# Moving VectorE's join to the head of its step, taking the edge spans apart amid the first keys, and zeroing the row table later

## What is computed

```python
xn = layernorm(x)
# graph part: mean over the incoming edges (sorted by dst), times W
h = segment_sum((xn @ W + b)[src], dst, N) / max(deg, 1)
# linear attention over all nodes, 8 heads
q, k = elu(xn @ wq + bq) + 1, elu(xn @ wk + bk) + 1
v = xn @ wv + bv
mix = ((q @ (k.T @ v)) / (q @ k.sum(0))) @ wo + bo
x = x + h + mix
# top-1 mixture of 8 experts, each with room for 977 rows
y = expert_of_argmax(softmax(layernorm(x) @ gate_w + gate_b))
x = x + y          # relu(x_e @ w1 + b1) @ w2 + b2, times the probability
```

## Time and profile before

| | |
|---|---|
| median of 3 runs | 1361.61 us (1361.3 to 1364.84) |
| the profiled execution, its own time | 1366.44 us |
| its span, first to last instruction | 1364.7 us |
| busy PE, VectorE, ACT, POOL | 1082.8, 821.7, 545.6, 918.9 us |
| mean granted TensorE clock | 0.918 |

### The profile page before, as it was taken

How to read it: one execution, slowest core, us unless ns; L and a number is a source line. 1 busy time by engine, 2 the same in 40 slices (tenths; PEclk the granted TensorE clock), 3 DMA queues, 4 the chain that set the end, 5 groups by cost and what they waited for, 6 DMA issues and landing times.

```text
span 1364.7 us, 31269 instructions
## 1 busy us (share of the span) xinstructions
PE 1082.8 (79%) x5701; PEld 775.4 (57%) x5702; DVE 821.7 (60%) x2770; ACT 545.6 (40%) x1411; POOL 918.9 (67%) x965
## 2 busy tenths in 40 slices
PE   3769986768767777878888888888888888888895
PEld 2446654435544545556555655666665666557785
DVE  6754433557657666657566666566666666667443
ACT  4832211223323333334244444355445444555442
POOL 4646777777777776777767777777776666651741
PEclk9569988788879898989799999899999999999998
DMA  7594333445445555556555565566666655653762
GB/s 231 179 287 133 102 105 107 144 120 154 149 143 157 151 159 172 154 154 191 155 178 185 176 185 181 164 205 191 183 185 189 201 174 168 180 177 109 241 208 82
DMA packets 141586, 228.92 MB, mean 168 GB/s; under 512 B 29601, under 2 KB 86594, under 8 KB 141489
## 3 DMA queue, kind: packets, MB, share of 16 engines
q0 software_dynamic: 42800, 115.65, 28.2%
q1 hardware_dynamic: 97454, 111.65, 26.4%
q10 hardware_dynamic: 1234, 0.66, 0.2%
HBM read 194.77 MB, written 34.81 MB: 168 GB/s over the span
## 4 chain that ended last, share of the span: by engine, by line
issue 24%; DVE 23%; PE 21%; POOL 14%; DVEq 8%; DMA 4%; ACT 3%; SPq 1%; POOLq 1%; ACTq 0%
POOL shared L600 13%; PE pA L943 4%; PE pY L1067 4%; PE pH L1076 4%; DVE shared L1451 2%; DMA shared<-table,idx 2%; DVEq L1399 2%; PE pH L917 2%; DVEq L1404 2%; DMA shared<-in_L_ffn_w_dram 1%; PE pQ L990 1%; PE pD L1004 1%; PE pT L998 1%; DVE stats L1524 1%; DVE shared L1585 1%
## 5 line engine op out<-in xcount | busy, mean ns | idle before, releaser
L600 POOL DMA_INDIRECT shared<-table,idx x784 | 765.9, 977 | 277.5 <-issue 238.9
L943 PE MATMUL pA<-shared,onehot 128*128 x976 | 264.4, 399 | 110.7 <-issue 53.1
L943 PEld LDWEIGHTS pA<-shared,onehot 128*128 x976 | 92.4, 99 | 262.9 <-issue 209.5
L1391 DVE TENSOR_TENSOR onehot<-tile_iota,dst_t 128x512 f32 x244 | 159.9, 694 | 101.8 <-PE pA L943 65.2
L1067 PE MATMUL pY<-w2s,shared 128*128 x832 | 197.3, 391 | 10.9 <-issue 10.6
L1076 PEld LDWEIGHTS pH<-shared 128*128 128x128 f32 x1664 | 193.9, 192 | 7.3 <-DMA shared<-in_L_ffn_w_dram 4.7
L1076 PE MATMUL pH<-shared 128*128 128x128 f32 x1664 | 195.2, 275 | 3.3 <-DMA shared<-in_L_ffn_w_dram 3.3
L1067 PEld LDWEIGHTS pY<-w2s,shared 128*128 128x128 f32 x832 | 157.1, 194 | 34.8 <-issue 14.5
L788 ACT ACTIVATE shared<-pH,b1s 128x128 f32<-128x128 f32 x416 | 116.5, 374 | 84.8 <-PE pH L1076 73.2
L1451 DVE RECIPROCAL shared<-shared 128x256 f32<-128x256 f32 x49 | 85.9, 1753 | 36.3 <-ACT shared L738 32.5
L558 POOL DMA_INDIRECT rows<-rows_sb,row_at x49 | 52.1, 1063 | 73.1 <-issue 72.5
(11 more groups left out here) (252 smaller groups left out, 1681.9 us busy)
## 6 DMA issues: line engine op xcount, KB each, us to landing
shared<-in_L_ffn_w_dram SPq DMA_DIRECT2D x104, 512.0 KB
shared<-table,idx POOLq DMA_INDIRECT x784
w2s<-in_L_ffn_w_dram SPq DMA_DIRECT2D x8, 1024.0 KB, 7.1
rows<-rows_sb SPq DMA_DIRECT2D x7, 1040.0 KB, 14.1
shared<-rows SPq DMA_DIRECT2D x52, 130.0 KB
shared<-in_L_ffn_b_dram SPq DMA_DIRECT2D x52, 128.0 KB
shared<-in_x_dram SPq DMA_DIRECT2D x12, 512.0 KB, 8.4
table<-w2s SPq DMA_DIRECT2D x12, 512.0 KB, 4.4
```

The costliest lines, as they stand in the source:

```text
L600: g.indirect_dma_start(gathered[:, s * G + j, :], None, table[:, :], bass.IndirectOffsetOnAxis(ap=idx[:, q * G % IDX + j:q * G % IDX + j + ...
L943: m = pe.matmul(pA[:, :], one_of[j][:, bass.ds(one, P)], got_of[j][:, bass.ds(got, 2 * D)], start=False, stop=final and j == G - 1)
L1391: v.tensor_tensor(onehot[:, n % OQ, :, :], tile_iota[:, :].rearrange("p (a n) -> p a n", a=1).broadcast_to([P, G, P]), dst_t[:, bass.ds(ch ...
```

## The change

It does four things. PE opens the first four gather groups as soon as the tiles are turned, projects three tiles, and only then takes part in the edge spans, now in pD and pA; VectorE does the keys of tiles 0 and 1 in the middle of that chain; tile 0's sum is set up at tile 9 of the keys, and VectorE's first one-hots come one at a time at tiles 7, 8 and 9 instead of four at once. SP issues the zeroing behind `bob` and `xres`, and VectorE waits for it at step 2. The join becomes a function of its own, ahead of `next_tile`.

```diff
# SP
+            sp.wait_ge(S["ms_ok"], 2)
+            sp.dma_start(bob, bo.partition_broadcast(P)).then_inc(S["bo_in"], 16)
+            sp.dma_start(xres, x_t[0, :, :]).then_inc(S["xr_in"], 16)
             sp.wait_ge(S["rows_z"], 2)
             for i in range(1, NX):
                 sp.dma_start(rows_t[...], empty...).then_inc(S["zeroed"], 16)
-            (the same three lines, here)
# PE
-            the span products in pX and pT; pe.wait_ge(S["spans_ok"], 1)
+            pe.sem_inc(S["slots"], FIRST)
...
-                sum_start(load_span(0))
-                sum_zero()
                 for t in range(KB - 1):
                     project(t)
+                the span products in pD and pA
                 for t in range(NT):
+                    if t == RING_X - 2:
+                        pe.wait_ge(S["spans_ok"], 1)
+                        sum_start(load_span(0))
+                        sum_zero()
# VectorE
             v.sem_inc(S["e_lohi"], 1)
+            v.wait_ge(S["tab_st"], 16 * BATCHES)
+            keys(0, 0)
+            keys(1, 1)
             v.wait_ge(S["e_rowps"], 1)
...
+                def join(t):
+                    v.wait_ge(S["ah_ok"], t + 1)
+                    hold(v, "dve_hold")
+                    v.tensor_tensor(ss[:, 0:D], pA[:, D:2 * D], ss[:, 0:D], ALU.add).then_inc(S["join_ok"], 1)
...
                         late()
+                    if joined(t):
+                        join(t)
                     if inner or t + 1 < NT:
                         next_tile(t)
...
-                load_ends(0)
-                early()
-                v.wait_ge(S["tab_st"], 16 * BATCHES)
-                for t in range(NT + 2):
+                for t in range(2, NT + 2):
+                    if t == 5:
+                        load_ends(0)
+                        v.reg_mov(mid_r, v.snap(first_r))
+                    if t in (7, 8, 9):
+                        some()
...
-                v.wait_ge(S["zeroed"], 16 * (NX - 1))
-                v.wait_ge(S["scat_done"], 16)
...
+                    if t == 2:
+                        v.wait_ge(S["zeroed"], 16 * (NX - 1))
+                        v.wait_ge(S["scat_done"], 16)
```

More of the change, by code:

```diff
@@ L362, in _ @@
                              empty.rearrange("p (a d) -> p a d", a=1).broadcast_to([P, JOBS, ROW])).then_inc(S["zeroed"], 16)
-            sp.wait_ge(S["ms_ok"], 2)
-            sp.dma_start(bob, bo.partition_broadcast(P)).then_inc(S["bo_in"], 16)
-            sp.dma_start(xres, x_t[0, :, :]).then_inc(S["xr_in"], 16)
             def load_res(i, last=False):
@@ L880, in _ @@
                     ins.then_inc(S["gc_ps"], 1)
[L883 to L894, removed]
             gp = (pH0, pH1)
@@ L902, in _ @@
             pe.wait_ge(S["w_late"], 16 * 4)
-            pe.wait_ge(S["spans_ok"], 1)
+            pe.sem_inc(S["slots"], FIRST)
             def project(t):
@@ L920, in _ @@
             pe.sem_inc(S["kv_used"], KB)
-            pe.sem_inc(S["slots"], FIRST)
             pe.sem_inc(S["oh_slots"], OQ - 1)
@@ L1129, in step @@
                         sum_rest()
-                sum_start(load_span(0))
-                sum_zero()
                 for t in range(KB - 1):
                     project(t)
+                pe.wait_ge(S["e_bound"], 1)
+                for a in range(2):
+                    ins = pe.transpose(pD[0:NT, a * P:(a + 1) * P], bounds[:, a, :], ident[:, :])
+                ins.then_inc(S["e_bt"], 1)
+                pe.wait_ge(S["e_lohi"], 1)
+                for a in range(2):
+                    ins = pe.matmul(pA[0:1, a * 64:a * 64 + NT], lohi[:, a:a + 1], ident[0:NT, 0:NT], start=True, stop=True)
+                ins.then_inc(S["e_rowps"], 1)
+                pe.wait_ge(S["e_row"], 1)
+                pe.matmul(pD[0:NT, 0:1], new_row[0:1, 0:NT], ident[0:1, 0:1], start=True, stop=True).then_inc(S["e_newps"], 1)
+                pe.wait_ge(S["e_new"], 1)
+                pe.matmul(pA[0:1, 0:NT], new_col[:, :], tri[0:NT, 0:NT], start=True, stop=True).then_inc(S["e_baseps"], 1)
                 for t in range(NT):
+                    if t == RING_X - 2:
+                        pe.wait_ge(S["spans_ok"], 1)
+                        sum_start(load_span(0))
+                        sum_zero()
                     if t + KB - 1 < NT:
@@ L1314, in _, with keys @@
             c(v.tensor_tensor(xgs[:, :, :], xgs[:, :, :], spread(gcon[:, 1, :]), ALU.add))
+            def keys(t, b):
+                v.wait_ge(S["k_ps"], t + 1)
+                c.mark(v.scalar_tensor_tensor(xgs[:, t, :], keys_ps(t)[:, D:GW], std[:, t:t + 1], xgs[:, t, :], ALU.mult, ALU.add))
+                v.tensor_tensor(kb[:, b, :], keys_ps(t)[:, 0:D], bks, ALU.add).then_inc(S["kb_ok"], 1)
             m0 = sel_f[:, 0:NT * EBLK].rearrange("p (t b) -> p t b", b=EBLK)
@@ L1335, in _ @@
             v.wait_ge(S["e_bt"], 1)
-            c.mark(v.tensor_reduce(lohi[:, 0:1], pX[0:NT, 0:P], AX, ALU.min))
-            c(v.tensor_reduce(lohi[:, 1:2], pX[0:NT, P:2 * P], AX, ALU.max))
+            c.mark(v.tensor_reduce(lohi[:, 0:1], pD[0:NT, 0:P], AX, ALU.min))
+            c(v.tensor_reduce(lohi[:, 1:2], pD[0:NT, P:2 * P], AX, ALU.max))
             c(v.tensor_scalar(lohi[:, 0:1], lohi[:, 0:1], BIG, float(EC - 1), ALU.add, ALU.min))
@@ L1346, in _ @@
             v.sem_inc(S["e_lohi"], 1)
+            v.wait_ge(S["tab_st"], 16 * BATCHES)
+            keys(0, 0)
+            keys(1, 1)
             v.wait_ge(S["e_rowps"], 1)
-            c(v.tensor_copy(lh_row[0:1, :, 0:NT], pT[0:1, 0:2 * 64].rearrange("p (a t) -> p a t", a=2)[:, :, 0:NT]))
+            c(v.tensor_copy(lh_row[0:1, :, 0:NT], pA[0:1, 0:2 * 64].rearrange("p (a t) -> p a t", a=2)[:, :, 0:NT]))
             c(v.scalar_tensor_tensor(new_row[0:1, 1:NT], lh_row[0:1, 1, 0:NT - 1], -1.0, lh_row[0:1, 0, 1:NT], ALU.add, ALU.is_gt))
@@ L1352, in _ @@
             v.wait_ge(S["e_newps"], 1)
-            c(v.tensor_copy(new_col[:, :], pX[0:NT, 0:1]))
+            c(v.tensor_copy(new_col[:, :], pD[0:NT, 0:1]))
             v.sem_inc(S["e_new"], 1)
             v.wait_ge(S["e_baseps"], 1)
-            c(v.tensor_scalar(base_row[0:1, 0:NT], pT[0:1, 0:NT], float(EQ), None, ALU.mult))
+            c(v.tensor_scalar(base_row[0:1, 0:NT], pA[0:1, 0:NT], float(EQ), None, ALU.mult))
             c.mark(v.tensor_tensor(new_row[0:1, 0:NT], lh_row[0:1, 1, 0:NT], lh_row[0:1, 0, 0:NT], ALU.subtract))
@@ L1366, in _ @@
             c(v.tensor_scalar(gcon[:, 0, :], gcon[:, 0, :], -1.0, None, ALU.mult))
[L1368 to L1371, removed]
             def features(t, b):
@@ L1498, in degrees @@
                     if joined(t):
-                        v.tensor_tensor(ss[:, 0:D], pA[:, D:2 * D], ss[:, 0:D], ALU.add).then_inc(S["join_ok"], 1)
                         v.wait_ge(S["join_ok"], t - T0)
```

## The result

| | before | after |
|---|---|---|
| median of the timed runs | 1364.27 us (1359.79 to 1367.62, 19 runs) | 1369.81 us (1364.8 to 1375.21, 19 runs) |
| the profiled execution, its span | 1366.44, 1364.7 us | 1368.11, 1366.4 us |
| mean granted TensorE clock | 0.918 | 0.924 |

The ratio after to before is 1.0042, 95% interval 1.0031 to 1.0054: by the ratio the change made the kernel 5.7 us slower, where 5.4 us faster was forecast. In time order, the profile after shows four things.

What follows compares the result with a forecast made beforehand. POOL's fetch stream was taken to bound the kernel up to 873 us, VectorE's own stream the late steps. The terms -2.1 + 2.7 - 7.6 + 1.6 = -5.4 us took the median 1361.61 to 1356.2, range 1347 to 1366.

Steps and rivals of the forecast that it cites:

- The front: Start of the kernel: PE opens the gather groups earlier, which feeds POOL sooner; 2.1 us gained, ends 4.2 and 0.
- The chain: At the start, from bounds turned (77.6) to spans ready (84.6), with two tiles' keys inside; first key sum at 85.7.
- the ring: Opened for POOL's fetches by tile 11's key sums; POOL's idle time there should end at about 111, not 112.93.
- the one-hots at tiles 7 to 9: At the start: VectorE needs 2.1 us for such a tile against 1.765, taking 1.0 us off the gain.
- The zeroing: Issued at about 236.56 - 2.1, it delays five groups' landings while POOL has no slack; 2.7 us lost, ends 0 and 5.
- Rival C: The zeroing is free, landings staying within 5 us, and the front pays in full: -10.2 us, 1351.4; chance 0.28.
- The join in the late steps: In 23 steps after 890 us, moving it saves VectorE 0.33 us each; 7.6 us gained, ends 0 and 13.3.
- Rival B: The late steps give nothing because the added wait stops VectorE's sequencer until the join is through: 1363.8; chance 0.18.
- the cover: In late steps, the join's 0.42 us of work runs beneath the register load of 0.79 us.
- The join in the waiting steps: Tiles 9 to 24: the register load queues behind the join, VectorE's work comes 1.0 us later; 1.6 us lost, ends 0 and 8.
- rival D: The register load behind the join costs PE 1.0 us in all 16 waiting steps: slower, +9 us, 1370.6; chance 0.12.

## Why the prediction was wrong

The sum was -5.4 us; +5.7 was measured. By its terms:

- **The front, 2.1 us gained** (ends 0 and 4.2): 5.2 us lost. This is the step that failed. The chain came out well: bounds turned at 76.74 (77.6 forecast), first key sum at 84.45 (85.7), the ring at 108.64 (110.8). What failed was the cost of "the one-hots at tiles 7 to 9", priced as VectorE time alone, 1.0 us. Three were made where the kernel before makes four; the number was not read as something that places all later ones. With four the front gains 2.7 us, a little over the forecast, so the missing one costs 7.9 us by the ratios, of which the profiles show 5.0 at `tile_iota` of tile 0 (249.68 against 244.72), 3.0 of them in the stretch of longer fetches. The ends were too narrow for this: a part that changes when an engine's work falls beside POOL's fetches needs a lower end below nothing.
- **The zeroing, 2.7 lost**: 3.5 by the ratio, in three landing waits, as described. The mechanism was right, the size 0.8 small. Rival C, which had it free, is refuted in the profile.
- **The join in the late steps, 7.6 gained** at 0.33 a step: 5.5 by the ratio, 0.17 to 0.23 a step in the profiles. The mechanism was right in kind. Two terms of the 0.33 are off: at its old place 0.42 was saved, not 0.48 (the next instruction waits 0.16 us: 1010.96 in the profile after), and in front it costs 0.23, not 0.15 (1.08 + 0.42 + 0.84 = 2.34 us up to `tile_iota`, against 2.11). Rival B is refuted: without the cover the join's whole 0.42 would have come on top of the 2.11.
- **The join in the waiting steps, 1.6 lost** (ends 0 and 8): 7.0. The delay of 1.8 us after the sum's end was right to 0.1, as was the register load behind the join as its cause: loading first takes most of the loss away. What failed is who waits. Three steps with a late fifth one-hot and one with a late row address were counted, at 1.0 us each; the wait at tile 14 alone grew by 1.3 to 1.6, and in tiles 9 to 12 PE also waits for VectorE's attention chain, which is on the same queue. It is rival D's mechanism, the register load behind the join, at 7 us instead of D's 16, but not by D's path: POOL waits by name for a row address only once there (2.9 us, in the run with the join ahead alone).

Alone the three parts make 5.2 + 3.5 + 1.5 = 10.2 us, together 5.7. The three intervals, some 2 us to either side each, make about 4 for their sum, so most of the difference of 4.5 can be scatter; that the parts overlap in time was not shown.

Rival D was named for "slower", with 0.12. Without the one-hots it would not have decided: -2.7 for the front, +3.5, +1.5 makes +2.3, within 0.3%. The sign came from a cause that no rival had.

## What to carry to other kernels

When work is made ahead in a ring of slots, count how many: one more or fewer decides whether the rest runs in lock-step with its consumer or free, and so what it falls beside. Take an instruction out of a step's tail into a gap that is there anyway, and keep a register load that used to run before a wait ahead of it: its place was worth some 5.5 us here. A step's head delays everything on its queue: look for each engine that waits for any of it, not only for the products that come first.

## What the hardware showed beyond the expected

**A fetch whose issue begins under a one-hot waits for the one-hot's end.** In the timelines of six of these kernels, from the ring's opening to 236 us, 74 fetches begin while a one-hot runs. Where the one-hot began 0.06 us or more before the fetch, the fetch ends 0.81 to 0.85 us after the one-hot's end, however long that makes it (up to 1.45 us), in all but six cases: five began in the last 0.1 us of the one-hot and took the 0.94 or 0.95 of a free fetch, and one was held on by the features' instruction that followed. In the profile after: 118.58 + 0.68 + 0.82 = 120.08, and the fetch ends at 118.64 + 1.44 = 120.08; 127.90 + 0.69 + 0.82 = 129.41 = 128.03 + 1.38. Where the one-hot began less than that before the fetch, or after it, the fetch takes its 0.95. When VectorE is idle as it begins, it takes 0.94 to 0.96 (56 fetches of the kernel after). The features' instruction, which also reads two operands from SBUF, holds a fetch in the same way (a third of some 80 took over 1.04 us; it is only 0.4 us long); the seven fetches of the kernel after that began under line 1318, which reads one operand from PSUM, took 0.95.

"SBUF — State Buffer" of the Trainium skill, section Who interferes with whom, says that a VectorE instruction with two inputs in SBUF contends with a GpSimd instruction that reads SBUF, and that the pair of ports is an exclusive lock for the whole instruction. The traces agree with it: the hold ends with VectorE's instruction, only a fetch that comes second is held, and an operand in PSUM avoids it. They don't show the lock the other way round: the one-hot of 128.14 above, which began under a fetch, took its 0.69 too. The page also infers that such an instruction doesn't stall the making of a DMA's descriptors, because only the write side is needed there. For an indirect DMA, which reads its indices from SBUF, the 0.49 us at 118.64 say otherwise, and the measurement decides.

The cost is small for one fetch and large in sum, because POOL is the bound: of some 98 fetches of the keys, 17 long ones instead of 8 make 3 us.
